# Gated cross-attention block with routed experts on one core: the last expert's output goes through ScalarE and is turned before its share is applied

## The reference

```python
x = x + tanh(g_xattn) * attention(layernorm(x), ctx)       # softmax over 6404 keys
y = layernorm(x)
routed = top2(softmax(y @ Wr + br)), divided by its sum    # 1024 x 8
h = relu(y @ W1[e] + b1[e])                                # 8 experts, 128 -> 512
expert_out = h @ W2[e] + b2[e]                             # 512 -> 128
x = x + tanh(g_ffn) * sum over e of routed[:, e] * expert_out[e]
```

## Time and profile before

| | us |
|---|---|
| Runs | 276.93, 275.99, 274.94 |
| Median | 275.99 |
| The profiled execution's own time | 274.55 |
| Its span, first to last instruction | 272.8 |
| Granted TensorE clock over the span | 0.999 |

### The profile page before, as it was taken

One profiled execution on the slowest core, in us unless ns is written; L12 is line 12 of the kernel. 1 busy time (PEld: TensorE's weight loads), 2 busy tenths in 40 slices (PEclk: granted clock), 3 DMA queues, 4 the chain that ended last, 5 costly groups with the idle time before them and its releaser, 6 DMA issues.

```text
span 272.8 us, 5070 instructions
## 1 busy us (share of the span) xinstructions
PE 266.0 (98%) x1662; PEld 245.4 (90%) x1662; DVE 210.5 (77%) x406; ACT 186.8 (69%) x338; POOL 109.3 (40%) x144
## 2 busy tenths in 40 slices
PE   7999999999999999999999999999999999999994
PEld 7677989999999999999889999999889998999993
DVE  4889977897486898789637478876688699467696
ACT  2997575445675556556577798888546664999990
POOL 3899993556800030000001553661025444355720
PEclk9999999999999999999999999999999999999999
DMA  6700020000099100000000222435301011313312
GB/s 191 275 2 0 0 82 0 2 1 2 0 248 338 42 0 2 0 1 2 1 0 2 77 77 79 117 126 145 106 15 37 24 32 35 91 58 73 86 53 81
DMA packets 18485, 17.08 MB, mean 63 GB/s; under 512 B 2410, under 2 KB 14940, under 8 KB 18460
## 3 DMA queue, kind: packets, MB, share of 16 engines
q1 hardware_dynamic: 17372, 15.31, 18.7%
q0 software_dynamic: 640, 1.31, 1.7%
q10 hardware_dynamic: 448, 0.14, 0.2%
HBM read 13.34 MB, written 3.42 MB: 61 GB/s over the span
## 4 chain that ended last, share of the span: by engine, by line
PE 87%; DVE 8%; DMA 2%; issue 1%; ACT 1%; SPq 1%; DVEq 0%
PE ps L1473 9%; PE ps L1499 9%; PE ps L1474 9%; PE ps L1500 9%; PE ps L1501 9%; PE ps L1475 9%; PE ps L1395 7%; PE ps L1600 4%; PE ps L1586 3%; DVE pmax L999 2%; DMA tok<-in_x_dram 2%; PE ps L1575 2%; PE ps L1625 2%; PE ps L1627 2%; PE ps L1626 2%; PE ps L1601 2%
## 5 line engine op out<-in xcount | busy, mean ns | idle before, releaser
L906 ACT ACTIVATE ex_hi<-ps 128x768 fp32r<-128x768 f32 (+1 forms) x78 | 56.9, 730 | 55.9 <-PE ps L1475 54.4
L1214 DVE TENSOR_TENSOR ex_lo<-ps,ex_hi 128x768 fp32r<-128x768 f32 (+1 forms) x66 | 58.4, 885 | 23.0 <-ACT ps L910 20.7
L999 DVE TENSOR_REDUCE pmax<-ps 128x1 f32<-128x512 f32 (+2 forms) x74 | 62.4, 874 | 10.3 <-PE ps L1395 9.5
L1499 PE MATMUL ps<-ex_hi,ctx_both 128*97 128x384 f32 (+1 forms) x153 | 49.7, 325 | 0.0
L910 ACT ACTIVATE ps<-ps 128x768 f32<-128x768 f32 (+1 forms) x66 | 49.7, 752 | 0.0
L1474 PE MATMUL ps<-q_lo,ctxT_hi 96*128 96x384 f32 (+1 forms) x153 | 49.0, 321 | 0.0
L1475 PE MATMUL ps<-q_hi,ctxT_lo 96*128 96x384 f32 (+1 forms) x153 | 48.6, 318 | 0.0
L1500 PE MATMUL ps<-ex_hi,ctx_both 128*96 128x384 f32 (+1 forms) x153 | 48.6, 318 | 0.0
L1501 PE MATMUL ps<-ex_lo,ctx_both 128*97 128x384 f32 (+1 forms) x153 | 48.6, 318 | 0.0
L1473 PE MATMUL ps<-q_hi,ctxT_hi 97*128 97x384 f32 (+1 forms) x126 | 42.3, 336 | 0.3 <-DVE ex_lo L1214 0.2
L1395 PE MATMUL ps<-ctxT_hi,q_hi 97*128 97x512 f32 (+1 forms) x104 | 34.3, 400 | 0.7 <-DVE pmax L999 0.4
(11 more groups left out here) (227 smaller groups left out, 545.2 us busy)
## 6 DMA issues: line engine op xcount, KB each, us to landing
raw<-in_ctx_dram SPq DMA_DIRECT2D x6, 384.0 KB, 6.1
w_raw<-in_L_ffn_W_dram SPq DMA_DIRECT2D x8, 256.0 KB, 3.9
raw<-in_L_ffn_W_dram SPq DMA_DIRECT2D x8, 256.0 KB, 6.3
raw<-in_L_ffn_b_dram SPq DMA_DIRECT2D x8, 256.0 KB
shared<-routing SPq DMA_DIRECT2D x8, 192.0 KB
x_slots<-shared SPq DMA_DIRECT2D x1, 1088.0 KB, 6.3
y_slots<-shared SPq DMA_DIRECT2D x17, 64.0 KB, 1.5
shared<-in_L_ffn_b_dram SPq DMA_DIRECT2D x1, 512.0 KB, 3.4
```

Of the source, the lines that this page charges most:

```text
L906: nc.scalar.activation(ex_pair(ex_hi, u % P_RING, js, n), scores, ACT.Exp)
L999: nc.vector.tensor_reduce(pmax[:, FIRST_TILE[ROUND_BLOCK[r]] + t, place:place + 1], max_home(s)[:, 0:w], AX.X, ALU.max).then_inc(max_reduc ...
L1214: nc.vector.tensor_tensor(ex_pair(ex_lo, u % P_RING, js, n), whole, ex_pair(ex_hi, u % P_RING, js, n).bitcast(F32), ALU.subtract).then_inc ...
L1499: nc.tensor.matmul(dst[0:CA, :], ch[:, j, :], hi, start=(j == first), stop=False)
```

## The change

The eighth expert (number 7) is no longer scaled by VectorE ahead of its turn. ScalarE brings its output plus the bias from the accumulator to on-chip memory in two parts, of 128 and 256 columns. TensorE turns each of the three tiles into a bank of its own, with a semaphore increment for each. With tokens on the partitions the share is a factor for each partition, so VectorE multiplies and adds in one instruction for each tile, with a factor `last_gain` = share times tanh(g_ffn), which one small new instruction makes. The two result DMAs stay as they are (two tiles, then one).

On TensorE the last `expert_out` now stands ahead of the turn of expert 6. On VectorE the scaling of expert 6 stands behind L1307 of unit 31, not ahead of it. The tenth gather sum moves from unit 30 to unit 29. The row of shares of expert 7 is no longer fetched.

```diff
-GATHER_UNITS = [24, 24, 25, 25, 26, 26, 28, 28, 29, 30]
+GATHER_UNITS = [24, 24, 25, 25, 26, 26, 28, 28, 29, 29]
 # SyncE
-            for e in range(2, E):
+            for e in range(2, E - 1):
                 fetch_routing(e)
 # ScalarE, after the last rectify
+            act.wait_ge(h_used, FU)
+            act.wait_ge(y_added, E - 3)
+            for columns_ in (slice(0, P), slice(P, SPAN)):
+                nc.scalar.activation(y_r[:, (E - 1) % 2, columns_], y_bank(E - 1)[:, columns_], ACT.Identity,
+                                     bias=cols[:, E * HC + E - 1:E * HC + E]).then_inc(last_out, 1)
             act.wait_ge(result_ready, len(END_PARTS))
 # VectorE, units
-                if u == FU - 1:
-                    scale_output(e - 1)
                 dve.wait_ge(h_ready, u + 1)
...
-                if u % HC == H_LAG and e > 0 and u < FU - 1:
+                if u % HC == H_LAG and e > 0:
                     scale_output(e - 1)
 # VectorE, end
+            step(nc.vector.tensor_scalar(last_gain[:, :], routed[:, LAST_TILES, E - 1], tanh_g[:, 1:2], None, ALU.mult))
             for piece, base in enumerate((tok, result)):
                 dve.wait_ge(sum_turned, piece + 1)
...
-            for part in range(len(END_PARTS)):
-                scale_output(E - 1, part)
-            for part, turned in enumerate(END_PARTS):
-                dve.wait_ge(y_turned, part + 1)
-                src = ps[:, part, 0:len(turned) * P].rearrange("p (t d) -> p t d", d=P)
-                ts = last_tiles(part)
-                nc.vector.scalar_tensor_tensor(out=result[:, ts, :], in0=src, scalar=tanh_g[:, 1:2],
-                                               in1=result[:, ts, :], op0=ALU.mult, op1=ALU.add).then_inc(result_ready, 1)
+            for t in range(SPAN_TILES):
+                dve.wait_ge(y_turned, t + 1)
+                at = FIRST_TILE[-1] + t
+                last = nc.vector.scalar_tensor_tensor(out=result[:, at, :], in0=ps[:, t, 0:P], scalar=last_gain[:, t:t + 1],
+                                                      in1=result[:, at, :], op0=ALU.mult, op1=ALU.add)
+                if t >= SPAN_TILES - 2:
+                    last.then_inc(result_ready, 1)
 # TensorE, end
-                if v == FU + H_LAG - 1:
-                    pe.wait_ge(y_scaled, E - 1)
-                    turn_expert(E - 2, range(SPAN_TILES), UB[0], sum_turned)
                 expert_out(v - H_LAG)
-            for part, turned in enumerate(END_PARTS):
-                pe.wait_ge(y_scaled, E + part)
-                turn_expert(E - 1, turned, ps[:, part, :], y_turned)
+            pe.wait_ge(y_scaled, E - 1)
+            turn_expert(E - 2, UB[0])
+            for t in range(SPAN_TILES):
+                pe.wait_ge(last_out, min(t + 1, 2))
+                nc.tensor.transpose(ps[:, t, 0:P], y_r[:, (E - 1) % 2, t * P:(t + 1) * P], ident[:, :]).then_inc(y_turned, 1)
```

More of the change, by code:

```diff
@@ L309, in attention_experts @@
         gain = sb("gain", [P, TOP, PLACED])
+        last_gain = sb("last_gain", [P, SPAN_TILES])
         r_dram = nc.dram_tensor("routing", [E, SPAN], F32).ap()
@@ L326, in attention_experts @@
         out_done = sem("out_done")
+        last_out = sem("last_out")
         ident_ready, pad_zeroed, ones_ready, earlier_ready, pool_step = sem("ident_ready"), sem("pad_zeroed"), sem("ones_ready"), sem("earlier_ready"), sem("pool_step")
@@ L439, in last_tiles @@
             return slice(FIRST_TILE[-1] + END_PARTS[part][0], FIRST_TILE[-1] + END_PARTS[part][-1] + 1)
-        def end_columns(part):
-            return slice(END_PARTS[part][0] * P, (END_PARTS[part][-1] + 1) * P)
         def step_at(b, i, name):
@@ L1271, in _, with scale_output @@
                     post(NB - 1, v)
[L1273 to L1283, removed]
+            def scale_output(e):
+                dve.wait_ge(h_used, (e + 1) * HC)
+                dve.wait_ge(r_b_in[e % 2], 16 * (e // 2 + 1))
+                if e == 0:
+                    dve.wait_ge(ys_summed, SLOT_TILES)
+                if e > 2:
+                    dve.wait_ge(y_added, e - 2)
+                dst = y_r[:, e % 2, :] if e else acc
+                nc.vector.scalar_tensor_tensor(out=dst, in0=y_bank(e)[:, 0:SPAN],
                                                scalar=cols[:, E * HC + e:E * HC + e + 1],
-                                               in1=r_b[:, e % 2, cut], op0=ALU.add, op1=ALU.mult).then_inc(y_scaled, 1)
+                                               in1=r_b[:, e % 2, :], op0=ALU.add, op1=ALU.mult).then_inc(y_scaled, 1)
             def gather_sum(k, t):
@@ L1674, in turn_sum, with turn_expert @@
                 last.then_inc(sum_turned, 1)
[L1676 to L1681, removed]
+            def turn_expert(e, bank):
+                for t in range(SPAN_TILES):
+                    last = nc.tensor.transpose(bank[:, t * P:(t + 1) * P], y_r[:, e % 2, t * P:(t + 1) * P], ident[:, :])
+                last.then_inc(sum_turned, 1)
             for v in range(LAG, SLOT_TILES):
```

## The result

The changed kernel has a median of 274.39 us, the kernel before 275.19 us, over 22 runs each; the ratio is 0.997 with a 95% interval of 0.9955 to 0.9984. The change makes the kernel faster by 0.8 us, and the interval is 0.44 to 1.24 us. The forecast was 0.64 us. Its level, 275.35 us, stood on the median of three runs, 275.99 us, which was 0.8 us above what more runs of the same kernel gave; the level came out high for that reason, the difference did not.

The account below looks back on a forecast made before the run. TensorE is busy nearly throughout, but VectorE's chain bounds the last 8 us. Dropped scalings and wait (0.74, 0.27 us), against 0.26 us for the factor and longer adds, save 0.64 us: 275.99 to 275.35 us, range 273.8 to 277.2 us.

Parts of the forecast that it names:

- What bounds the end: Last 8 us: the end of VectorE's last adds counts, a sum of its instructions plus a 0.27 us idle wait.
- T: Time from the start of VectorE's scaling of expert 5 to the last result DMA's issue; that issue forecast 0.64 us earlier.
- Rival 3: The end hangs on something the change leaves alone, or the gain is lost on VectorE: 276.0 us, chance 0.09.
- The terms: End of VectorE: scalings (0.74 us) and wait (0.27) go, factor adds 0.26, last adds 0.86 for 0.74: -0.63 us.
- The fixed time behind the last issue: From the later result DMA's issue to the span's end: 2.16 us, unchanged.
- The moved sum: Tenth gather sum ahead of unit 30's L1307: TensorE's expert_out of unit 30 starts 0.03 us later.
- The turn of expert 6: On TensorE behind the last matmul: takes 0.55 us, ends 0.15 us ahead of VectorE's second L1318.
- The spare time of ScalarE's path: Expert 7's turned tiles are ready before VectorE's last adds, with 0.40, 0.29 and 0.43 us to spare.
- Rival 2: ScalarE late after the last matmul, as by a 1.28 us table load: slower, 276.4 us, chance 0.05.
- Rival 1: VectorE's last adds do not lap, or the turn of expert 6 is late: gain 0.48 or 0.40 us, chance 0.21.
- The late turn: Half of Rival 1: the turn of expert 6 keeps VectorE waiting 0.08 us before the second L1318.
- The level: Forecast time of the whole changed kernel: 275.99 us, the median of three runs, less 0.64 us, 275.35 us.

Follow-up runs that it names:

- The order alone: Kernel before with only the new orders on VectorE and TensorE, expert 7 still scaled by VectorE: ratio 1.0009 to the kernel before, 0.26 us longer at the end.
- the early factor: Changed kernel with last_gain made in unit 8 instead of at the end: ratio 0.9978 to the kernel before, 6.92 us from scaling of expert 5 to last issue.

## Why the prediction was right

- **What bounds the end.** The forecast said that the end is VectorE's sum behind unit 30. It holds in the changed kernel, T falling by 0.63 us against 0.64 us. The order alone, with an earlier last matmul and a later end, shows it best. Rival 3, that nothing moves, falls by the interval of the gain, 0.44 to 1.24 us.
- **The terms.** The two copies on ScalarE took 0.37 us and 0.47 us (0.36 and 0.47 forecast), the factor 0.21 us (0.23), the three adds 0.87 us together (0.86). The fixed time behind the last issue came out at 273.1 - 271.04 = 2.06 us (2.16).
- **The moved sum.** Costed at 0.03 us on TensorE and nothing at the end. The run with the sum back in unit 30 has the same T within 0.02 us; on TensorE the move cost 0.06 us.
- **The turn of expert 6.** Given 0.15 us to spare, it had none. Two sizes were off: after a wait TensorE's three matmuls of unit 30 took 0.64 us (267.73 to 268.37) and not 0.53 us, and from the turn to VectorE it takes 0.10 us, not 0.03 us; the turn itself, 0.49 us for 0.55 us, gave some of it back. The result did not show it, because the two paths now end together; the early factor did, by gaining nothing. That the forecast came out within 0.01 us is in part luck: a slightly later turn would have been paid in full.
- **The spare time of ScalarE's path.** Forecast 0.40 us at tile 0 and 0.29 us at tile 1, with tile 1 the tighter. With one activation more VectorE waited at tile 0 already: the adds start at 269.36 us, where its own sum would have had them at 269.08 us (268.43 + 0.62 + 0.03). Of the 0.47 us, 0.19 us were hidden there and 0.16 us over the whole end. The last matmul was 0.10 us later than forecast, and the 0.10 us from a turn to VectorE counts here too. Rival 2's mechanism is real: three activations more and the kernel is slower than before. It did not occur on its own, as no second table load appeared.
- **Rival 1.** The three adds lapped, each 0.345 us long and the three 0.87 us, although waits stand between them. Without a lap they would have taken 1.04 us (3 x 0.345 us). The Trainium skill, page "VectorE: DVE Perf Modes", section "The DRAIN you can't avoid", has both: the next instruction waits for an empty pipeline, and one that is not held starts earlier. The rows agree with the second. The late turn, the other half of this rival, is real and was short of showing by about 0.01 us.
- **The level.** The 275.35 us was 1 us too high, 0.8 us of it from a median of three runs. The allowance for that in the range was needed. The 2.8 us of a change of 1% is 3.8 times the largest term of the sum (0.74 us), not over four times; nothing hangs on it.

## What to carry to other kernels

When two executions of nearly the same kernel are compared, fix a common instruction just ahead of the change and measure from there: a span can grow by 0.3 us while the edit gains 0.6 us. Moving work off an engine pays only down to the next path that ends there, so sum up both paths, with 0.1 us for a restart after a wait, before the next saving is made; here 0.26 us more off VectorE gave nothing. Two edits may only pay together: the earlier last matmul cost 0.26 us with the old route and was worth 0.30 us with the new one.

## What was not expected of the hardware

A 128-column sum with two operands in on-chip memory takes 0.34 us on VectorE, but 1.72 us and 1.77 us when it met a row fetch issued by GpSimd and the add behind it. The Trainium skill, page "GPSIMD Engine Reference", section "Key points", says that GpSimd shares its interfaces to that memory with VectorE, with contention where a VectorE instruction has two inputs there; the rows agree, and show the loser held until the other's add has ended. The add alone is enough (0.81 us for a sum that started inside one), and the issue of a fetch alone was not (0.34 us for a sum inside one). Why the two long ones were held although they started 0.5 and 0.6 us ahead of the add is open. The same shows in the kernel before at a smaller size, 1.11 us for a pair.
